# A mask over all sixteen vectors in place of strikes, new places in the turns, and values folded into one weight product

## The reference, cut to what matters

```
# branch s: three attentions over xn, gated, projected, normalised
v   = rows @ Wv + bv                    # for the windows, the blocks and the selected rows
out = concat([comp * g0, sel * g1, win * g2]) @ Wo + bo
s   = layernorm(out * 0.5 + xn * 0.5)

# branch f: product keys, 8 heads
sim = (xn @ Wq.T) . keys                # 16 vectors (2 sides x 8 heads) of 32 scores per row
sx, sy = top 16 of 32 of each vector
scores = top 16 of the 256 sums sx[i] + sy[j]
f   = sum over the 16 chosen of gelu(x . W_down) * softmax(scores) * W_up
```

## Time and profile before

| what | value |
|---|---|
| median of 3 runs | 282.97 us (282.95 to 283.81) |
| profiled execution | 282.19 us, its span 280.4 us |
| DVE busy | 269.0 us, 96% of the span |
| PE busy | 239.2 us, 85% |
| ACT busy | 236.1 us, 84% |
| POOL busy | 225.1 us, 80% |
| DVE strikes (L1151, both instructions) | 512 pairs |
| granted TensorE clock, mean | 0.994 |

### The profile page before, as it was taken

One profiled execution on the slowest core, in us unless ns is written; L12 is line 12 of the kernel. 1 busy time (PEld: TensorE's weight loads), 2 busy tenths in 40 slices (PEclk: granted clock), 3 DMA queues, 4 the chain that ended last, 5 costly groups with the idle time before them and its releaser, 6 DMA issues.

```text
span 280.4 us, 7939 instructions
## 1 busy us (share of the span) xinstructions
PE 239.2 (85%) x1562; PEld 174.1 (62%) x1562; DVE 269.0 (96%) x2579; ACT 236.1 (84%) x1048; POOL 225.1 (80%) x344
## 2 busy tenths in 40 slices
PE   7899797887888798979898889888888888889891
PEld 7566243674667576667576657665666666667690
DVE  6899989999999999999999999999999999999885
ACT  2555768699888999899989998999899989997853
POOL 7889610577688889997999799988998899888772
PEclk9999999999999999999999999999999999999997
DMA  7930000000000000100010001000000001000102
GB/s 174 281 75 2 0 1 0 0 4 0 5 1 0 5 1 0 42 1 1 4 39 4 1 1 39 5 0 2 12 28 5 0 1 39 4 2 4 37 4 75
DMA packets 11235, 6.29 MB, mean 22 GB/s; under 512 B 1457, under 2 KB 10674, under 8 KB 11186
## 3 DMA queue, kind: packets, MB, share of 16 engines
q1 hardware_dynamic: 9858, 5.12, 6.9%
q10 hardware_dynamic: 1328, 0.66, 1.2%
HBM read 3.67 MB, written 2.10 MB: 21 GB/s over the span
## 4 chain that ended last, share of the span: by engine, by line
DVE 70%; PE 11%; issue 7%; ACT 5%; POOL 4%; DMA 2%; SPq 1%; DVEq 0%; POOLq 0%
DVE rest L1151 26%; DVE top L1160 15%; DVE top L1140 14%; DVE last L1184 6%; PE s_bank L1502 2%; DVE slot_gap L1169 2%; DMA x_sb<-in_L_attn_hidden_states 2%; PE f_bank L1509 1%; PE c_bank L1509 1%; PE scratch L1496 1%; DVE slot_gap L1175 1%; DVE nmax L1236 1%; POOL squareT L494 1%; PE t_bank L1465 1%; PE t_bank L1537 1%
## 5 line engine op out<-in xcount | busy, mean ns | idle before, releaser
L1151 DVE MATCH_REPLACE8 rest<-top,sim 128x32 f32<-128x32 f32 x512 | 85.8, 179 | 0.1
L1160 DVE MAX8 top<-rest 128x8 f32<-128x32 f32 x512 | 53.5, 177 | 0.7
L831 ACT ACTIVATE prob<-drop 128x50 f32<-128x50 f32 x224 | 51.6, 256 | 0.0
L1140 DVE MAX8 top<-sim 128x8 f32<-128x32 f32 x496 | 50.9, 178 | 0.0
L831 ACT ACTIVATION_READ_ACCUMULATOR prob<-drop 128x1 f32 x224 | 47.0, 214 | 0.0
L1151 DVE MATCH_VALUE_LOAD rest<-top,sim 128x8 f32 x512 | 40.8, 80 | 0.3
L479 POOL TENSOR_TENSOR past<-gap,last 128x400 f32<-128x400 f32 x31 | 26.8, 863 | 11.4 <-DVE last L1184 11.3
L494 POOL TENSOR_TENSOR squareT<-sideT 100x512 bf16<-100x512 bf16 x31 | 32.2, 1040 | 3.5 <-ACT sideT L741 3.5
L1519 PE MATMUL sim<-sim_w,xT_all 128*128 128x512 f32 x64 | 33.4, 604 | 0.5 <-ACT xT_all L778 0.5
L507 POOL TENSOR_TENSOR wgt<-prob,rden 128x400 f32<-128x400 f32 x30 | 25.7, 856 | 7.9 <-DVE rden L1130 7.9
L501 POOL TENSOR_TENSOR drop<-gap,out_by 128x400 f32<-128x400 f32 x30 | 31.0, 1034 | 0.5 <-ACT out_by L730 0.5
(11 more groups left out here) (292 smaller groups left out, 720.9 us busy)
## 6 DMA issues: line engine op xcount, KB each, us to landing
out<-y_sb SPq DMA_DIRECT2D x7, 256.0 KB, 2.3
x_sb<-in_L_attn_hidden_states SPq DMA_DIRECT2D x2, 256.0 KB, 3.8
fwq_sb<-in_L_ffn_Wq ACTq DMA_DIRECT2D x2, 256.0 KB, 5.9
x_sb<-in_L_attn_hidden_states SPq DMA_DIRECT2D x1, 512.0 KB, 5.4
wc_sb<-in_L_attn_Wc SPq DMA_DIRECT2D x1, 256.0 KB
out<-last_y SPq DMA_DIRECT2D x2, 128.0 KB, 1.9
wo_in<-in_L_attn_Wo SPq DMA_DIRECT2D x1, 192.0 KB
keys_sb<-in_L_ffn_keys ACTq DMA_DIRECT2D x1, 128.0 KB, 3.4
```

Of the source, the lines that this page charges most:

```text
L831: last = nc.scalar.activation(prob[d][:, h, :], drop[:, h, :], ACT.Exp, scale=-1.0, accum_out=den[d][:, h:h + 1])
L1140: last = nc.vector.max(top[d][:, v, 0:8], sim_bank[d][:, bass.ts(v, KEYS)])
L1151: last = nc.vector.match_replace(out=rest[:, v, :], in_to_replace=top[d][:, v, 0:8], in_values=sim_bank[d][:, bass.ts(v, KEYS)], imm_value ...
L1160: last = nc.vector.max(top[n % 2][:, v, 8:16], rest[:, v, :])
```

## The change

It finds the second 8 in another way. `mark_above` compares all 16 vectors with their 8th largest value in one instruction of 512 columns and writes 1 or 0. `strike_above` adds -1e38 where the mark is 1, again in one instruction. Where several scores equal the 8th value, more than 8 are marked; so `sum_above` counts the marks of each vector (into the used score bank in PSUM), `spill_above` turns the counts into eight slots for each vector, and `put_ties` fills a slot with the 8th value for each score marked too many. `rest` has 40 columns for each vector, 32 and the 8 slots, and `next_8` reads all 40.

```diff
-            def strike_8(n, q):
...
+            def mark_above(n):
+                dve.wait_ge(sim_top8, n + 1)
+                if n >= 1:
+                    dve.wait_ge(summed_above, n)
+                nc.vector.tensor_tensor(above[:, :, :], sim_bank[n % 2][:, :].rearrange("p (v k) -> p v k", k=KEYS),
+                                        eighth(n, KEYS), ALU.is_ge).then_inc(above_done, 1)
+            def strike_above(n):
+                dve.wait_ge(above_done, n + 1)
+                if n >= 1:
+                    dve.wait_ge(top_done, 2 * n)
+                nc.vector.scalar_tensor_tensor(rest[:, :, 0:KEYS], above[:, :, :], STRUCK,
+                                               sim_bank[n % 2][:, :].rearrange("p (v k) -> p v k", k=KEYS),
+                                               ALU.mult, ALU.add).then_inc(struck, 1)
+            def sum_above(n):
+                dve.wait_ge(struck, n + 1)
+                nc.vector.tensor_reduce(sim_bank[n % 2][:, 0:TIES], above[:, :, :], AX_X, ALU.add
+                                        ).then_inc(summed_above, 1)
+            def spill_above(n):
+                dve.wait_ge(summed_above, n + 1)
+                nc.vector.scalar_tensor_tensor(tie_slots(n),
+                                               sim_bank[n % 2][:, 0:TIES].unsqueeze(2).to_broadcast([P, VECS, 8]), 2.0,
+                                               rank_row[:, 7:15].unsqueeze(1).to_broadcast([P, VECS, 8]),
+                                               ALU.mult, ALU.subtract).then_inc(spill_done, 1)
+            def put_ties(n):
+                dve.wait_ge(spill_done, n + 1)
+                nc.vector.scalar_tensor_tensor(rest[:, :, KEYS:KEYS + 8], tie_slots(n), SPILL, eighth(n, 8),
+                                               ALU.mult, ALU.min).then_inc(sim_used, 1)
```

`above` is bf16, and `top` has three buffers where it had two. DVE's turn n now begins with the strike of tile n; the first 8 and the mark of tile n+1 are done inside it:

```diff
             def turn(n):
                 b, j = divmod(n, TB)
+                strike_above(n)
+                if n + 1 in tiles:
+                    first_8(n + 1, [0])
+                sum_above(n)
                 if j == 0:
                     maxima(b - 1)
...
+                invert_sums(n - 4)
+                spill_above(n)
+                if n + 1 in tiles:
+                    first_8(n + 1, [1])
+                put_ties(n)
+                if n + 1 in tiles:
+                    mark_above(n + 1)
+                next_8(n, 0)
+                gaps_of_pairs(n - 1)
+                if j == 0:
                     inverse_row_sums(b - 1)
+                next_8(n, 1)
+                gaps_of_thirds(n - 1)
+                if n < TILES - 1:
                     last_gaps(n - 1)
```

```diff
+            def turn_values():
+                pe.wait_ge(w_late, 16 * LATE_DMAS)
+                pe.wait_ge(wo_step, 4)
+                nc.tensor.transpose(f_bank[:, 0:D], wv_sb[:, :], ident[:, :])
+                mm(f_bank[0:1, D:4 * D], bv_sb[:, 0:1], wo_sb[:, :, :].rearrange("p r d -> p (r d)"),
+                   start=True, stop=True).then_inc(values_in, 1)
+            def fold_values():
+                pe.wait_ge(bvo_done, 1)
+                mm(f_bank[:, D:4 * D], wvT[:, :], wo_sb[:, :, :].rearrange("p r d -> p (r d)"),
+                   start=True, stop=True).then_inc(values_folded, 1)
...
             product.then_inc(z_ready, 1)
+            scores(3)
+            turn_values()
             top_columns(1)
             pair_gaps(1)
-            scores(3)
+            fold_values()
             places_matrix()
...
+            sp.wait_ge(bvo_done, 1)
+            for r in range(3):
+                for j in range(TB):
+                    sp.dma_start(vww[WKEYS + r:WKEYS + r + 1, j, :], bvo[:, r, :]).then_inc(bo_put, 16)
...
             take_topT(1)
+            act.wait_ge(values_in, 1)
+            nc.scalar.activation(wvT[:, :], f_bank[:, 0:D], ACT.Copy)
+            nc.scalar.activation(bvo[:, :, :], f_bank[0:1, D:4 * D].rearrange("p (r d) -> p r d", r=3),
+                                 ACT.Copy).then_inc(bvo_done, 1)
             side_of(0)
             take_gaps(1)
+            act.wait_ge(values_folded, 1)
+            nc.scalar.activation(wvo[:, :, :], f_bank[:, D:4 * D].rearrange("p (r d) -> p r d", r=3),
+                                 ACT.Copy).then_inc(wvo_done, 1)
...
+                nc.gpsimd.tensor_copy(p_win[:, :, WKEYS:WROWS],
+                                      gates[:, :, :, bass.ds(b, 1)].rearrange("p g t a -> p t (g a)"))
...
+                        if j % LAST == 0:
+                            mm(out_bank[:, bass.ds(j * D, LAST * D)], ident[:, :],
+                               xn_all[:, bass.ds(b * TB + j, LAST), :].rearrange("p t d -> p (t d)"),
+                               start=True, stop=False)
```

More of the change, by code:

```diff
@@ L196, in program @@
         qw = sb("qw", [P, L])
[L197 removed]
+        kw = sb("kw", [P, WTOK])
         csT = sb("csT", [P, CS])
[L199 to L201 removed]
+        qcs, kcs = (sb(n, [P, CS]) for n in ("qcs", "kcs"))
+        vww = sb("vww", [WROWS + 1, TB, D])
         vwc = sb("vwc", [P, 2, D])
@@ L213, in program @@
         s_norm = [sb(f"s_norm{i}", [P, TB, D]) for i in range(2)]
-        top = [sb(f"top{i}", [P, VECS, TOPK]) for i in range(2)]
-        rest = sb("rest", [P, VECS, KEYS])
+        top = [sb(f"top{i}", [P, VECS, TOPK]) for i in range(3)]
+        above = sb("above", [P, VECS, KEYS], BF16)
+        rest = sb("rest", [P, VECS, KEYS + 8])
         topT = sb("topT", [P, 2 * P])
@@ L1130, in invert_sums, with first_8 @@
                 nc.vector.reciprocal(rden[d][:, :], den[d][:, :]).then_inc(rden_done, 1)
[L1132 to L1136, removed]
+            def first_8(n, halves=range(2)):
+                if n >= 3:
+                    dve.wait_ge(topT_ready, n - 2)
                 dve.wait_ge(sim_ready, n + 1)
-                for h in range(2):
-                    for v in range(h * HALF_V, (h + 1) * HALF_V):
-                        last = nc.vector.max(top[d][:, v, 0:8], sim_bank[d][:, bass.ts(v, KEYS)])
+                for v in range(HALF_V * halves[0], HALF_V * (halves[-1] + 1)):
+                    last = nc.vector.max(top[n % 3][:, v, 0:8], sim_bank[n % 2][:, bass.ts(v, KEYS)])
+                if 1 in halves:
@@ L1324, in _ @@
-            for n in range(TB):
-                first_turn(n)
+            first_turns()
             for n in range(TB, TILES):
@@ L1732, in turn @@
                     block_values_out(b - 1)
+                    if n + 2 in tiles:
+                        scores(n + 2)
                     count_places(n - 2)
@@ L1836, in _ @@
                     pair_gaps(0)
-                    scores(2)
                     expert_parts()
@@ L1851, in _ @@
                     transpose_gates()
+                    pe.wait_ge(wvo_done, 1)
+                if b == 4:
+                    scores(4)
                 hidden(b)
@@ L1869, in _ @@
             project_pairs(0)
+            scores(5)
             for n in range(TB, TILES):
```

251 lines of the change are left out of this document (112 added, 139 removed).

## The result

The changed kernel took 281.93 us (median of 20 runs, 279.65 to 284.76), the kernel before beside it 283.44 (20 runs, 282.54 to 285.55); the ratio of the two is 0.993, 95% interval 0.9905 to 0.995. So it is faster by 0.7%, some 2 us where 6.2 were forecast, and the median is above the range. One thing has to be known to read the runs: every ratio leaves out the runs that took over 1.5% more than the fastest run of their kernel (here three, 284.24 to 284.76 us; further on 362.95 and 649.84 in e1, 282.96 in e3 and 529.61 in e4). The time goes with TensorE's mean granted clock: the three runs with a mean of 0.990 or more took 279.65, 279.84 and 279.86 us, and the others, at 0.985 or less, 281.4 and up. The profiled execution (282.02 us, span 280.1, mean clock 0.985) is one of the latter.

What follows compares the result with a forecast made beforehand. DVE, busy 96% of the span, was taken to bound the kernel. 282.2 + 1.4 (start-up) - 5.3 (turns) - 1.5 - 0.4 (tail) = 276.4, as a median 276.8 us; range 270.5 to 281.6, the forecast's own 273 to 280.5.

Steps and rivals of the forecast that it cites:

- DVE's steps: New DVE instructions in each turn: 0.60 us per 512 column one, 0.20 per 128 column one, 2.20 us a turn.
- Rival (2): Wide DVE instructions paid whole, at 0.69 and 0.28 us: 0.15 us more a turn, 286.1 us in all; chance 0.12.
- Four turns of 27.7 us and 0.3 of stalls: Steady turns: DVE's four turns fall from 28.8 to 27.7 us, less 0.3 of new stalls; net gain 0.8.
- Rival (1): In the turns the neighbours ACT and POOL take the pace: four turns some 28.6 us, 280.8 in all; chance 0.12.
- I take 1.2 us more at `maxima`: Start-up: new PE and ACT work makes the first maxima 1.2 us later, bounds 0 and 3.4.
- I take 1.5 (bounds 0 and 2.17), and 0.4: Tail: DVE gets back 1.5 us of work done ahead; 0.4 more from the value product and eviction that go.
- The upper end of the range: Whole kernel: the forecast's own range ends at 280.5 us, for 0.8 of stalls in four turns and start-up at 3.4.

Runs made afterwards that it cites:

- e1: The changed kernel with the score product of tile 4 moved from the loop of hidden products back behind the key projection; 281.15 us, ratio to before 0.990.
- e3: The changed kernel with the two products of the folded values and their copies moved from ahead of the hidden products to behind the key projection; 280.15 us (0.985).
- e4: The changed kernel with the reciprocal of the softmax row sums moved to the end of the first turn of four; 285.09 us (1.005).
- e10: The changed kernel with the mask kept but its steps following one another in a tile's own turn, nothing of the next tile between; 299.61 us (1.057).
- e8: e3 with three unused TensorE products ahead of the counting in every turn; 284.60 us, ratio to the kernel before 1.005.
- e2: The changed kernel with eight unused TensorE products in the idle stretches between 51 and 55 us; 280.66 us (0.990).
- e9: e3 with, in the last batch alone, block projection and block scores earlier and the pairs' projection ahead of the window scores; 277.17 us (0.977).

## Why the prediction was wrong

- *DVE's steps: right.* Steps of 0.60 and 0.20 were taken, 0.59 and 0.19 came. Rival (2), steps paid whole, is what happens without cover, and costs more than it was priced at: 0.73 and 0.33 in e10, where 0.69 and 0.28 were put. The places are that cover.
- *Four turns of 27.7 us and 0.3 of stalls: right in the sum, by luck in its parts.* DVE's own steps make 27.3 (3 x 6.64 and 7.39), 0.4 less than forecast; the stalls are 0.8, 0.5 more; together 28.15, a gain of 0.70 against 0.8. From maxima 0 to 6 it was 5.34, because the first group of four turns went at DVE's own 27.33. Rival (1) is near: e4 and e8 made the neighbours the pace with little.
- *"I take 1.2 us more at `maxima`": the step that failed first.* It was 4.90. Two parts of that had no term at all. One is TensorE's clock, 2.16 us (e2): the prediction did not ask what TensorE was left with further on, where it took the third window product and `scores(4)` out. TensorE stood idle there for half of 4 us, and its clock halved behind that. That the idleness caused it is likely and not shown for each execution. The other is `scores(2)` ahead of the logits, 0.87 (35.01 in e3 for 34.14), shown by the trace alone. What the term did name, the fold ahead of the hidden products and `scores(4)` among them, makes the rest, 1.87 for the 1.2: 1.30 is the fold (e3), and the 0.57 left is near the 0.67 that e1 gives `scores(4)`. Without the clock the lateness is 2.74 (62.67 in e2), more than twice the 1.2 but within the bounds of 0 and 3.4.
- *"I take 1.5 (bounds 0 and 2.17), and 0.4": the step that failed second.* DVE did get its hand back (2.86 us earlier with turn 31, 0.44 of them already at maxima 6), and it bought 0.26 at the scores of batch 7. The prediction's own reservation was the answer: "the other engines still have their own work in that turn". TensorE's counting of tile 29, ahead of those scores, waits for GpSimd and starts within 0.03 us of where it did before, and DVE had waited only 0.36 us for the scores there. So this chain stood right behind DVE's. With the chain shortened (e9) the end came 1.4 us earlier by the stretches and 1.7 by the lowest runs. The 0.4 for the values' last product and eviction did not show: maxima 7 to the end is 20.30 for 20.34.
- *The upper end of the range.* It is said to stand for 0.8 of stalls in four turns and a start-up at 3.4. Those give 282.2 + 3.4 + 0.2 - 2.1 - 1.9 = 281.8 (2.1 is 6.5 times 1.12 less 0.8), not 280.5. The range was too narrow by the prediction's own bounds, and the measured start went beyond even those.
- By stretches the error is +3.7 us up to maxima 0 (4.9 for 1.2), -0.7 over the 24 turns (-5.34 for 0.2 - 4.8) and +2.5 behind them (+0.14 for -0.5 - 1.9), with the 0.13 outside the span 5.6: from 276.4, the sum, to 282.0.

## To carry to other kernels

What one engine gains is worth only the distance to the next chain in that place: look up who is late next in the first and last turn by themselves, where the steady turns say nothing. Go through every product that the change moves, the small ones too, and follow the chain that it now stands in. Where a change takes work from TensorE ahead of a chain that TensorE paces, look whether it now idles there, and at the granted clock of the microseconds that follow. An instruction that is cheap by its width is cheap only with another between it and its reader.

## Not expected of the hardware

- A clock that falls for some 6 us in the start costs 2.16 us at maxima 0 and 2.2 at the end (the profiled executions of the changed kernel and of e2). The Trainium skill ("TensorE: Matmul & The Clock Gate", Part 1: The HAM clock gate) says that the clock goes by how busy TensorE has been, with two levels alone; the rows agree with 0.50 and 1.00, the idle microseconds standing ahead of the 0.50.
- A wait of DVE on its own last result costs 0.13 us a step whether the instruction is 0.69 or 0.29 us long (0.73 against 0.59, 0.33 against 0.20), some 0.6 us a turn in e10. The Trainium skill ("VectorE: DVE Perf Modes", The DRAIN you can't avoid) says of a chain of copies that "the semaphore costs nothing extra here"; e10 is another case, since the waits stand in both kernels and only the instructions between a result and its reader are gone.
